# Attention of each batch by halves of the queries, with its side work dealt anew

## The reference, cut to what matters

```python
w  = _rigid_transform(x, shift, angle)             # bilinear, per batch
Q, K, V = (w @ WQ + bQ), (w @ WK + bK), (w @ WV + bV)       # 16 heads x 16
A  = softmax(where(causal, Q K^T / 4, -1e5))       # 1024 x 1024 per head and batch
x1 = x + (A V) summed over the heads @ WO + 16 * bO          # WO is (16, 256)
y  = zX * lap_x(x1) + zY * lap_y(x1) + zR * x1 * (1 - x1)    # second differences, reflected ends
logits = y @ W_router + b_router                   # 8 experts, top 2, softmax of the two
out = x1 + sum_e weight_e * (relu(y @ W1[e] + b1[e]) @ W2[e] + b2[e])     # 256 -> 1024 -> 256
```

## Time and profile before

| | |
|---|---|
| three runs | 954.56, 941.21, 953.87 us; median 953.87 us |
| the profiled execution | 950.23 us, span 948.4 us |
| mean granted TensorE clock | 0.889 of full speed |
| PE, DVE, ACT, POOL busy | 74%, 50%, 38%, 33% of the span |
| stages in the trace (us from the span's start) | warp and projection of batch 0 to about 223, first maxima to 250, attention 250 to 599, early tiles 599 to 707, the other tiles to the end |

### The profile page before, as it was taken

One profiled execution on the slowest core, in us unless ns is written; L12 is line 12 of the kernel. 1 busy time (PEld: TensorE's weight loads), 2 busy tenths in 40 slices (PEclk: granted clock), 3 DMA queues, 4 the chain that ended last, 5 costly groups with the idle time before them and its releaser, 6 DMA issues.

```text
span 948.4 us, 14765 instructions
## 1 busy us (share of the span) xinstructions
PE 703.7 (74%) x4659; PEld 488.7 (52%) x4659; DVE 471.5 (50%) x1013; ACT 359.9 (38%) x912; POOL 312.0 (33%) x292
## 2 busy tenths in 40 slices
PE   0441222365678888988899998899869999999992
PEld 0341111142234343534345542788759999989881
DVE  6435555597575776475777774446411221211210
ACT  0121333254367754446364557312203233222320
POOL 1103454485698842200110006302622112111112
PEclk9866555586599999989999999899989999999997
DMA  6999888689763303996911003767879999899961
GB/s 216 301 270 313 279 285 284 226 281 329 206 240 118 113 2 115 282 333 226 368 73 47 1 2 124 264 232 220 291 228 331 316 328 329 280 354 379 342 165 22
DMA packets 136208, 216.17 MB, mean 228 GB/s; under 512 B 10357, under 2 KB 102058, under 8 KB 135978
## 3 DMA queue, kind: packets, MB, share of 16 engines
q1 hardware_dynamic: 114808, 150.78, 48.1%
q0 software_dynamic: 16784, 61.51, 20.9%
q10 hardware_dynamic: 4546, 3.08, 1.1%
HBM read 160.87 MB, written 56.37 MB: 229 GB/s over the span
## 4 chain that ended last, share of the span: by engine, by line
DMA 34%; PE 29%; DVE 17%; issue 8%; POOL 7%; ACT 2%; SPq 1%; DVEq 1%; POOLq 1%; ACTq 0%
DMA results<-arena,home 13%; DMA result<-arena,home 7%; DVE arena L1730 7%; PE psum L1433 5%; PE psum L1262 5%; DMA table<-arena 4%; PE psum L1447 3%; PE psum L1495 3%; PE psum L1504 3%; DMA arena<-table,tap_col 3%; POOL pairs_x L1018 2%; DMA arena<-qk_rows 2%; POOL arena L883 2%; PE psum L1396 2%; PE psum L1275 2%
## 5 line engine op out<-in xcount | busy, mean ns | idle before, releaser
L1182 ACT ACTIVATE arena<-psum 128x512 f32<-128x512 f32 (+3 forms) x384 | 170.5, 492 | 133.5 <-PE psum L1452 95.8
L1730 DVE TENSOR_REDUCE arena<-psum 128x2 f32<-128x1024 f32 (+2 forms) x192 | 176.2, 954 | 64.7 <-PE psum L1268 50.6
L1232 ACT ACTIVATE arena<-psum,b_cols 128x128 f32<-128x128 f32 x312 | 84.7, 382 | 234.8 <-PE psum L1495 234.8
L1495 PE MATMUL psum<-arena 128*128 128x128 f32 x1248 | 150.5, 280 | 6.5 <-issue 3.6
L1495 PEld LDWEIGHTS psum<-arena 128*128 128x128 f32 x1248 | 149.1, 197 | 9.7 <-issue 8.1
L1504 PE MATMUL psum<-arena 128*128 128x256 f32 x624 | 143.5, 384 | 10.7 <-DVE arena L2062 10.7
L1262 PE MATMUL psum<-arena 96*128 96x512 bf16 (+3 forms) x384 | 109.7, 352 | 32.4 <-DMA arena<-qk_rows 16.9
L1504 PEld LDWEIGHTS psum<-arena 128*128 128x128 f32 x624 | 116.9, 192 | 26.7 <-issue 12.0
L1447 PE MATMUL psum<-arena 99*128 99x512 bf16 (+3 forms) x384 | 113.8, 334 | 13.9 <-ACT arena L1182 8.2
L2058 DVE TENSOR_TENSOR arena<-psum,arena 128x256 f32<-128x256 f32 x39 | 16.6, 424 | 159.6 <-PE psum L1504 85.5
L1262 PEld LDWEIGHTS psum<-arena 96*128 96x128 bf16 x384 | 35.3, 102 | 105.0 <-DVE arena L1730 52.8
(11 more groups left out here) (212 smaller groups left out, 907.6 us busy)
## 6 DMA issues: line engine op xcount, KB each, us to landing
arena<-L_ffn_W SPq DMA_DIRECT2D x78, 1024.0 KB, 7.4
pairs_x<-zeros SPq DMA_DIRECT2D x4, 4160.0 KB, 25.5
arena<-qk_rows SPq DMA_DIRECT2D x16, 768.0 KB, 11.2
table<-arena SPq DMA_DIRECT2D x20, 384.0 KB, 9.6
qk_rows<-arena SPq DMA_DIRECT2D x16, 384.0 KB, 5.4
arena<-pairs_x SPq DMA_DIRECT2D x39, 130.0 KB, 6.5
qk_rows<-arena SPq DMA_DIRECT2D x16, 256.0 KB, 5.7
padded<-arena SPq DMA_DIRECT2D x2, 1328.0 KB
```

The source lines that it names most:

```text
L1182: nc.scalar.activation(probs[at % 2][h][:, q0:512], banks[turn % SCORE_BANKS][:, q0:512], ACT.Exp, scale=DH ** -0.5).then_inc(exp_done, 1)
L1232: ins = nc.scalar.activation(hidden_t[k % SLOTS][:, f], banks[hidden_bank(k) + f // 4][:, (f % 4) * P:(f % 4 + 1) * P], ACT.Relu, bias=b1_ ...
L1495: ins = t_.matmul(banks[first + f // 4][:, (f % 4) * P:(f % 4 + 1) * P], w1_slot[u][:, c, f * P:(f + 1) * P], x_t[:, c], start=c == 0, sto ...
L1730: return v.reduce_max(part[:, 2 * pair:2 * pair + 2, qb], psum[:, first:first + 2, 0:keys], AX_X)
```

## The change

The unit of attention is no longer a group but a batch, a half of the queries and a group (`UNITS`, 16 of them). For each batch the lower halves of all four groups come first (four steps each), then the upper halves (eight steps each). The number of steps stays 96. What follows from it:

- `stacks` is laid out by half, `chunk_place` is reordered so that chunks 0 to 3 are the lower rows of Q and K, and `load_stack` loads a unit (two DMAs of half the size).
- The maxima are kept by unit: 8 pairs for a lower unit, 16 for an upper. Only unit 0's 8 pairs are made ahead of `turn_max`; unit 1's follow as a prelude; `deal_pairs` deals the other 176 over steps 0 to 85, about two a step. `turn_max` is done 16 times, three steps ahead of its unit.
- `weighted` reads V in place (`v_all`) with 17 columns in place of the padded 32; `group_of_v`, `v_group` and ACT's zeroing go.
- Of batch 1's eight chunks the first four get their second and third part from DVE, in the side job itself. The projections stand at steps 21 to 24 and 40 to 43.
- ACT's and DVE's waits for two blocks of batch 1's warp ahead of attention go, and the steps of that warp are moved (`TURN_AT`, `HATS_AT`).
- Batch 0's routing stands at steps 49 to 74, the choice at step 72 and `rank` at step 74, with pairs of units 14 and 15 after it in DVE's order. A part of batch 1's routing moves into attention: one `turn_z`, two `attend`, one `lap`, one `turn_du`, one `logits`, and `turn_b1`. `LAST_PLAN` has 14 jobs, and its `rank` directly follows the last `logits`.
- SP's order is rewritten: after the store of chunks 0 to 3 the loads of units 0 to 3, then the store of chunks 4 to 7, then `store_neg(0)`; the clears of `pairs_x` and the loads of later units stand between later `store_neg`; the experts' weights are loaded as the last units free the stacks.

```diff
-STEPS = [(1, 0), (1, 7), (1, 1), (1, 6), (1, 2), (1, 5), (1, 3), (1, 4), (0, 0), (0, 3), (0, 1), (0, 2)]
-NS = len(STEPS)
+UNITS = [(b, half, g) for b in range(NB) for half in range(2) for g in range(NG)]
+KEY_TILES = [[0, 3, 1, 2], [0, 7, 1, 6, 2, 5, 3, 4]]
+UNIT_AT = [0]
+for _b, _half, _g in UNITS:
+    UNIT_AT.append(UNIT_AT[-1] + len(KEY_TILES[_half]))
+ALL_STEPS = [(u, s) for u, (_b, _half, _g) in enumerate(UNITS) for s in range(len(KEY_TILES[_half]))]
+UNIT_PAIRS = [[(pair, r) for r in (0, 1, 2, 3) for pair in range(2)],
+              [(pair, r) for r in (7, 5, 4, 6, 9, 8, 10, 11) for pair in range(2)]]
+CHUNKS = len(UNIT_PAIRS[0])
+LEAD = 3
...
-HATS_AT = {4: (0, 3), 5: (0, 8), 6: (1, 1), 7: (1, 6)}
-TURN_AT = [(0, 0), (0, 1), (0, 2), (0, 6), (0, 11), (1, 4), (1, 10), (2, 2)]
-PROJECT_AT = [(2, 4), (2, 5), (2, 6), (2, 7), (2, 8), (2, 9), (2, 10), (2, 11)]
-VALUES_AT = [(3, 0), (3, 0), (3, 1), (3, 1)]
-TURN_STEP = 8
+HATS_AT = {3: 5, 4: 11, 5: 17, 6: 22, 7: 27}
+TURN_AT = [1, 4, 14, 20, 25, 30, 35, 39]
+PROJECT_AT = [21, 22, 23, 24, 40, 41, 42, 43]
+VALUES_AT = [25, 26, 44, 44]
+FIRST_ROWS = 2
...
-    return j // 2 % 2, j // 4, j % 2
+    return j % 2, j // 2 % 2, j // 4
...
+        def deal_pairs(plan):
+            def step_us(t):
+                u, s = ALL_STEPS[t]
+                b, half, g = UNITS[u]
+                return HG * (0.17 + 0.00082 * (512 - max(KEY_TILES[half][s] * P - half * 512, 0)))
+            due = [UNIT_AT[u] - LEAD for u in range(len(UNITS))]
+            loaded = ([0] * 2 * NG + [UNIT_AT[NG + g + 1] + 4 for g in range(NG)]
+                      + [UNIT_AT[2 * NG] + 4 + g for g in range(NG)])
+            begin = [max(loaded[u], due[u - 2]) if u >= 4 else 0 for u in range(len(UNITS))]
+            left = [(u, pair) for u in range(2, len(UNITS)) for pair in UNIT_PAIRS[UNITS[u][1]]]
+            def pair_us(job):
+                return 0.2 + 0.002 * chunk_of(job[1][1])[2]
+            over = 0.0
+            for t in range(len(ALL_STEPS)):
+                rate = max([sum(pair_us(job) for job in left if job[0] <= u) / sum(step_us(k) for k in range(t, due[u]))
+                            for u in range(2, len(UNITS)) if due[u] > t and any(job[0] <= u for job in left)] + [0.0])
+                over += rate * step_us(t)
+                while left and begin[left[0][0]] <= t and (over >= pair_us(left[0]) / 2 or t == due[left[0][0]] - 1):
+                    u, pair = left.pop(0)
+                    over -= pair_us((u, pair))
+                    plan[t].append(("pair", pair, u))
+                if left and begin[left[0][0]] > t:
+                    over = 0.0
+            assert not left
+            for u in range(2, len(UNITS)):
+                plan[due[u]].insert(0, ("turn_max", 0, u))
+            plan[0].insert(0, ("turn_max", 0, 1))
...
+                plan[UNIT_AT[u] + 2].insert(0, ("sum", 0, u - 1))
+            t0 = UNIT_AT[len(UNITS) // 2]
+            for what, i, t in ([("turn_z", 0, 1), ("turn_z", 1, 3)] + [("attend", i, 4 + i) for i in ROW_ORDER]
+                               + [(what, i, t) for (what, i), t in
+                                  zip(ROUTE_PLAN, (11, 12, 14, 15, 16, 17, 18, 19, 20, 21, 23, 24, 26))]):
+                plan[t0 + t].append((what, i, 0))
+            t0 = UNIT_AT[len(UNITS) - NG]
+            for what, i, t in ([("turn_z", 0, 4)] + [("attend", i, 6 + i) for i in ROW_ORDER[:FIRST_ROWS]]
+                               + [("lap", 0, 16), ("turn_du", 0, 18), ("logits", 0, 20), ("turn_b1", 0, 22)]):
+                plan[t0 + t].append((what, i, 1))
...
-        LAST_PLAN = ([("attend", i, 1) for i in ROW_ORDER[0:2]] + [("sum", 0, 2 * NG - 1), ("turn_z", 0, 1)]
-                     + [("attend", i, 1) for i in ROW_ORDER[2:4]] + [(what, i, 1) for what, i in ROUTE_PLAN])
+        LAST_USES = FIRST_USE + len(PRELUDE) + sum(len(uses) for uses in ATTENTION)
+        LAST_PLAN = ([("sum", 0, len(UNITS) - 1), ("turn_z", 1, 1)] + [("attend", i, 1) for i in ROW_ORDER[FIRST_ROWS:]]
+                     + [("lap", i, 1) for i in (1, 2, 3)]
+                     + [("turn_du", 1, 1), ("turn_du", 2, 1), ("logits", 1, 1), ("turn_du", 3, 1), ("logits", 2, 1),
+                        ("logits", 3, 1), ("rank", 0, 1)])
...
+                    for c in range(2):
+                        parts_are_stored(b, 0, c)
+                        for u in (2 * c, 2 * c + 1):
...
+            store_neg(0)
+            for c in range(2):
+                parts_are_stored(0, 1, c)
+                for g in (2 * c, 2 * c + 1):
+                    load_stack(NG + g)
+            for u in range(1, 6):
+                store_neg(u)
...
+            clear_pairs(0)
+            store_neg(6)
+            for c in range(2):
+                parts_are_stored(1, 0, c)
...
+            store_parts(1, range(PART_SLOTS, QK_CHUNKS))
             clear_pairs(2)
+            store_neg(2 * NG)
+            unit_done(NG + 3)
+            load_stack(2 * NG + 3)
+            store_neg(2 * NG + 1)
+            for c in range(2):
+                parts_are_stored(1, 1, c)
+            load_stack(3 * NG)
+            store_neg(2 * NG + 2)
+            store_neg(2 * NG + 3)
+            for g in range(1, NG):
...
+            unit_done(3 * NG)
             load_w1(0)
+            load_w1(1)
+            store_neg(3 * NG + 2)
+            unit_done(3 * NG + 1)
+            load_w1(2)
+            load_w2(0)
+            store_neg(3 * NG + 3)
+            unit_done(3 * NG + 2)
+            load_w2(1)
...
+            ones_beside(1)
+            for j in range(PART_SLOTS, QK_CHUNKS):
...
+                    ins = t_.matmul(banks[OUT_BANK][32 * h:32 * h + DH + 1, q0:512], v_all[:, b, kt, g * HG + h],
+                                    probs[t % 2][h][:, q0:512], start=s == 0, stop=s == len(KEY_TILES[half]) - 1)
...
+            for use in PRELUDE:
+                side(*use)
...
+                    own = i < PART_SLOTS
+                    rest = resid[1 if own else i % 2]
                     dve.wait_ge(first_parts, n + 1)
-                    dve.wait_ge(parts_ready, n - 1)
-                    v.scalar_tensor_tensor(out=resid[i % 2], in0=bank, scalar=bqk[:, kind, c:c + 1],
+                    dve.wait_ge(parts_ready, n if own else n - 1)
+                    v.scalar_tensor_tensor(out=rest, in0=bank, scalar=bqk[:, kind, c:c + 1],
                                            in1=parts[i % PART_SLOTS][:, 0], op0=ALU.add,
                                            op1=ALU.subtract).then_inc(max_read, 1)
+                    if own:
+                        dve.wait_ge(max_read, use + 3)
+                        v.tensor_copy(parts[i][:, 1], rest).then_inc(halved, 1)
+                        dve.wait_ge(halved, n + 1)
+                        v.tensor_tensor(parts[i][:, 2], rest, parts[i][:, 1], ALU.subtract).then_inc(parts_ready, 1)
```

More of the change, by code:

```diff
@@ L110 @@
 ROW = D + 4
[L111 to L112 removed]
+ROW_ORDER = (0, 1, 2, 3)
+LAP_ORDER = (0, 1, 2, 3)
 NEG = -1.0e30
@@ L313, in build @@
         z_t = region(LATE_AT)([S])
-        max_parts = region(ARENA - PROJECTION_WORDS - 2 * HG * SB)([2, HG * SB])
+        z_halves = [[z_t[:, half * 512:(half + 1) * 512] for half in range(2)],
+                    [region(MIX_AT)([512]), z_t[:, 512:1024]]]
+        max_parts = region(ARENA - PROJECTION_WORDS - 4 * HQ)([2, 2, HQ])
         late_at = ARENA - PROJECTION_WORDS + SB * H * (DH + 1)
@@ L413, in build @@
         parts_stored = [sem(f"parts_stored{u}") for u in range(PART_SLOTS)]
-        stack_in = [sem(f"stack_in{g}") for g in range(NG)]
+        stack_in = [[sem(f"stack_in{half}{g}") for g in range(NG)] for half in range(2)]
         v_ready = sem("v_ready")
-        v_group_ready = sem("v_group_ready")
         scored = sem("scored")
@@ new lines, in attention_plan @@
+        def attention_plan():
+            plan = [[] for t in ALL_STEPS]
+            deal_pairs(plan)
+            for k, t in enumerate(TURN_AT):
+                plan[t].append(("turn_w", k, 1))
+            for j, t in enumerate(PROJECT_AT):
+                plan[t].append(("project", j, 1))
+            for j, t in enumerate(VALUES_AT):
+                plan[t].append(("values", j, 1))
+            for u in range(1, len(UNITS)):
+                plan[UNIT_AT[u] + 2].insert(0, ("sum", 0, u - 1))
[8 more added lines that the diff above has]
+                plan[t0 + t].append((what, i, 1))
@@ L920, in gather @@
                 if k == 3:
-                    for slot in range(PART_SLOTS):
-                        pool.wait_ge(parts_stored[slot], PART_STORES * 2)
+                    pool.wait_ge(v_ready, 2)
                 if k >= 2:
@@ L970, in add_up, with ones_beside @@
                 g_.sem_inc(late_mixed, 1)
+            def ones_beside(half):
+                rows = slice(half * SB // 2, (half + 1) * SB // 2)
+                g_.memset(v_all[:, 1, rows, :, DH:DH + 1], 1.0).then_inc(v_cleared, 1)
             def second_batch(fast):
```

(29 more changed lines are left out.)

405 lines of the change are left out of this document (158 added, 247 removed), and 4 rows, old and new, of the table EARLY.

## The result

The changed kernel takes 972.45 us (median of four runs, 969.5 to 979.58), the kernel before, run beside it, 948.62. The ratio is 1.0266 with a 95% interval of 1.0159 to 1.0374: slower by 2.7%. The forecast was 945 with a range up to 972 and the other sign. The profiled execution took 972.87 us with a span of 971.1, 22.7 more than the span of before.

A forecast was written before the change was run, and what follows sets the result against it. Attention was taken as bound by PE's work plus its waits for DVE and the DMA queue. 950.2 - 12 (start) + 15 (attention) - 12 (after) = 941.2; with 3.6 from profiled run to median, 945 us, range 918 to 972.

The forecast's parts named there:

- The start: Ahead of attention: the first score comes at 238 instead of 250, 12 us earlier, with bounds of 17 and 3.
- The dealing gives back 12: In attention: pairs dealt two a step instead of three cost less each, saving 12 us of PE's waits, at least 5.
- Six of PE's 12.6 us lie beside DVE's work: In attention: of PE's 12.6 us of added work, 6 are covered by DVE's long work in steps 68 to 86.
- The queue's wait of 5 us goes: In attention: PE's one 5.1 us wait for copied maxima of a later group disappears, counted as -5.
- The placing costs 10: Late in attention: pairs of units 14 and 15 wait behind DVE's placing of rows, costing 10 us (0 to 15).
- Four chunks on DVE, 3 us: In attention's side job: casts and subtractions for four batch 1 chunks on DVE cost 3 us (0 to 10), partly hidden.
- The wait for unit 8's maxima, 6 us: At step 48: these maxima, issued behind the third clear of routed rows, arrive late and cost 6 us (0 to 13).
- After attention: From attention's end onward: five fewer jobs and an earlier second scatter save 12 us (3 to 18).
- DVE sets the pace: Rival, in attention: DVE's jobs outlast PE's scores and jobs, attention grows 48 us, time 978 us; chance 0.15.
- No earlier start: Rival, ahead of attention: unit 0's maxima wait for loads and stores, attention begins at 250, time 957 us; chance 0.11.
- The side work disappears: Rival, in attention: side work hides between the scores, attention takes 8 us less, time 922 us; chance 0.25.
- Seventeen columns don't run side by side: Rival, in attention's weighted products: the eight instructions run in a row, 198 us more, time 1143 us; chance 0.04.

The follow-up runs named there:

- the late rank: The changed kernel with batch 0's rank at step 86 instead of 74, behind the last pair, and two late units' maxima issued earlier: 972.22 us, ratio 1.0291.

## Why the prediction was wrong

**The start.** The mechanism was named, the queue, and its size was off. DVE was ready earlier than I put it (first maxima at 221.8 against 228 to 231), and the copies landed later (244 against 237): I took the transfers at the stretch's mean rate and left out that SP must first have issued all twelve stores. -5.7 stands between my -12 and the bound of -3. That the whole 12 was to be had at the start the runs show (229.3, 231.4); that it would have been a gain of 12 they deny, since batch 0 then takes 5 us more (204.0 against 198.9, though the wait before unit 8 is gone there).

**Attention, the step that failed.** The sum was 7 - 12 + 6 + 10 + 3 + 6 - 5 = +15; measured is +35.5, inside the bounds of -8 to +45 that I had set. (The ends of the terms as I stated them add up to -20 and +55, not to -16 and +60.) Three terms failed, all of them gains or cover that I took off: the dealing's 12, six of PE's work, and the five of the queue.

- *The dealing gives back 12.* It gave nothing that the trace shows. I read PE's 12.1 us before pairs as an effect of three pairs a step. With two a step they are 19.5, of which 6.15 belong to the placing. Unit 6 does eight steps with 16 pairs in 29.4 us; with 18.0 for the steps and some 2.8 for its four other jobs a pair costs 0.54 by this estimate, not the 0.44 that I took from group 6 before.
- *Six of PE's 12.6 us lie beside DVE's work.* Mostly they do not: the run that took the early routing out of attention made it 5.4 us shorter, so those jobs, some 6 us by my prices, had little cover. PE's working time grew by 20.4, not 7. By the estimate from busy time and clock some 10 of it are more work, near the 12.6 that I had counted and then partly taken off; the other 10 are the lower clock, which stood nowhere in my sum. The windows of the earlier trace rows showed it as a mean of 0.97 over attention.
- *The queue's wait of 5 us goes.* It was never in attention: the 5.1 us of the earlier trace rows end at 250.0 with the first score, and the chain of the earlier trace rows holds them too. I counted them once in the start and once more here.
- *The placing costs 10.* Right in size: 10.7 in unit 13 by the late rank. I had put it down to PE's standing still alone; 4.8 of it are the lower clock.
- *Four chunks on DVE, 3 us.* Both prices came, as said: cast and subtraction take 0.43 and 0.69 us in three of the four, 0.71 and 2.18 in one; what PE felt of it was not measured. The Trainium skill's rule (SBUF — State Buffer, "Who interferes with whom"), told in the prediction, agrees with the trace: POOL was adding when that one began, and when none of the other three did.
- *The wait for unit 8's maxima, 6 us.* It is 3.7, and behind the clear as said: with the clear moved it goes.

With the dealing and the queue at 0, PE's work at 12.6, the placing at 10.7 and unit 8's wait at 3.7 my own terms give 12.6 + 6 + 10.7 + 3 + 3.7 = 36. That this meets the 35.5 is in part luck: the 6 for `turn_max` and the 3 for the chunks were not measured, and the lower clock outside unit 13 is in no term.

**After attention.** -7.1 in place of -12. The second scatter starts 12 us sooner (I had put 9), but tile 9 only 8. From the scatter's start to tile 9 PE works 44.8 us in the changed kernel and 37.0 before: products of the early tiles that are still to be made come in between. The run with the routing put back shows that 5.5 of the gain are the five jobs themselves, and they are paid for in attention.

**The rivals.** *DVE sets the pace* had the right sign, and it came to be in part: it is true of unit 13 (DVE 32.5 us of 41.5) and not shown for attention as a whole (PE's waits for DVE grew by 14 us of the 35, and halving the reductions closes 8). *No earlier start* is half true. *The side work disappears* is refuted. *Seventeen columns don't run side by side* is refuted by one row of the changed kernel, which answers to the earlier trace rows:

```profile
372.50 1.05 PE L1447 MATMUL psum<-arena 128*17 128x512 f32 x8
```

The Trainium skill's sentence that a column tile's output is the 32 partitions of a strip (TensorE: Matmul & The Clock Gate, "What picks the tile position") need not be read as a demand for all 32: with 17 columns at the first partition of each strip the eight products take 1.05 us, with 32 they took 1.06.

**What stays open.** Of the 35.5 us, 10.7 are the placing, 5.4 the early routing and 3.7 the wait before unit 8, each by a run that took it away. For the other 16 I have only the trace: the rest of PE's added work, the lower clock outside unit 13, longer waits for DVE, and the counts, eight more pairs and eight more `turn_max` in attention. A few us of it can be the difference between two executions. No run took these alone, and the even dealing was not set against three pairs a step in the same kernel.

## What to carry to other kernels

A wait that was taken out of the front of a queue with one written order stood at its next entry: before moving one copy ahead, list who else is behind the same transfers, and try small, urgent copies on another queue. A wait belongs to the stage in which it stands: before crediting one to a stage, look up which instruction it ends with. A long run of small operations on the engine that reads PE's side work cost more than PE's longest stop (10.7 us in unit 13, the stop 6.15), since part of the work there ran at a lower clock. It belongs where no side work is queued behind it, and its consumer (here a scatter of 20 us) sets how late that may be. Work that was moved from one PE-bound stage to another gained nothing (5.4 us less, 5.5 more).

## What was not expected of the hardware

The clock's part: in unit 13, around PE's stop of 6.15 us, the granted clock was 0.79, and PE worked 30.8 us; with the same work in pieces and no such stop 0.87 and 29.8; without the placing 0.94 and 26.0. It also differs between executions where the program is the same: ahead of unit 13 PE worked 264.7 us at 0.95 in the changed kernel and 259.4 at 0.97 with the late rank. And a small copy's landing depends on its queue: issued behind 3 MB of loads on SP's queue, 4 KB copies kept PE waiting 18.2 us, and the score came 13.5 us after the last of them was issued; on ACT's queue, with the same loads under way, PE waited 2.7 and 3.4 us, and in the second case the score came 6.5 us after the issue.
